# Adding the experts' weighted rows in DRAM by accumulating scatters, in a fused two-layer kernel

## What is computed

```python
logits = flat @ router_w.T                       # 1024 tokens, 32 experts
scores = jnp.sqrt(jax.nn.softplus(logits))
_, idx = jax.lax.top_k(scores + expert_bias, 4)  # four experts per token
topv = jnp.take_along_axis(scores, idx, axis=1)
topv = topv / (topv.sum(axis=-1, keepdims=True) + 1e-20)
...
out = sum over experts e of p[:, e, None] * _clamped_swiglu(flat, gate_w[e], up_w[e], down_w[e])
out = out + _clamped_swiglu(flat, shared_gate_w, shared_up_w, shared_down_w)
```

## Time and profile before

| | before |
|---|---|
| median of 3 runs | 845.72 us (844.31 to 847.45) |
| the profiled execution | 846.73 us |
| its span (first to last instruction) | 844.9 us |
| PE, DVE, ACT, POOL busy | 787.4, 605.4, 465.3, 429.8 us |
| mean granted TensorE clock | 0.993 of full speed |
| read from and written to DRAM | 41.11 MB, 21.86 MB |

### The profile page before, as it was taken

One profiled execution on the slowest core, in us unless ns is written; L12 is line 12 of the kernel. 1 busy time (PEld: TensorE's weight loads), 2 busy tenths in 40 slices (PEclk: granted clock), 3 DMA queues, 4 the chain that ended last, 5 costly groups with the idle time before them and its releaser, 6 DMA issues.

```text
span 844.9 us, 14053 instructions
## 1 busy us (share of the span) xinstructions
PE 787.4 (93%) x4927; PEld 642.0 (76%) x4927; DVE 605.4 (72%) x1069; ACT 465.3 (55%) x822; POOL 429.8 (51%) x487
## 2 busy tenths in 40 slices
PE   7999999998888988899899999999999999999993
PEld 6776776774333376798798899889989999888881
DVE  8588868658999787789788688986777544445544
ACT  4433342379888643786665566556656725555421
POOL 1767837423555455455245435757565415555423
PEclk9999999999999999999999999999999999999997
DMA  5211195000000040000000000101011887543134
GB/s 184 76 38 38 38 288 145 1 1 1 1 1 2 16 132 13 20 11 22 7 19 7 26 7 20 51 25 58 18 46 33 240 303 268 165 133 101 27 101 149
DMA packets 50117, 59.82 MB, mean 71 GB/s; under 512 B 13560, under 2 KB 41085, under 8 KB 50049
## 3 DMA queue, kind: packets, MB, share of 16 engines
q1 hardware_dynamic: 45488, 50.49, 19.4%
q0 software_dynamic: 4560, 8.44, 2.8%
HBM read 41.11 MB, written 21.86 MB: 75 GB/s over the span
## 4 chain that ended last, share of the span: by engine, by line
PE 55%; DVE 9%; ACT 7%; POOL 7%; issue 5%; DMA 1%; SPq 0%; POOLq 0%; ACTq 0%; DVEq 0%
PE ps L801 12%; PE ps L516 8%; PE ps L518 8%; PE ps L517 8%; PE ps L894 4%; PE ps L891 3%; PE ps L925 3%; POOL A L1814 2%; DVE cap L1509 2%; PE ps L712 2%; POOL rot L1845 2%; PE ps L873 1%; PE ps L558 1%; ACT A L1108 1%; DVE swap L1499 1%
## 5 line engine op out<-in xcount | busy, mean ns | idle before, releaser
L801 PE MATMUL ps<-V,P 128*128 128x129 f32 x1152 | 150.7, 276 | 0.0
L1160 ACT ACTIVATE cap<-cap 128x1024 f32<-128x1024 f32 (+7 forms) x128 | 87.1, 681 | 113.7 <-DVE cap L1509 108.1
L801 PEld LDWEIGHTS ps<-V,P 128*128 128x128 f32 x1152 | 143.3, 192 | 2.7
L1509 DVE SCALAR_TENSOR_TENSOR cap<-dist,ps 128x1024 f32<-128x1024 f32 (+7 forms) x128 | 95.4, 750 | 27.9 <-PE ps L518 20.4
L1738 POOL TENSOR_SCALAR_AFFINE_SELECT P<-P 128x128 f32<-128x128 f32 x128 | 39.0, 305 | 144.4 <-ACT P L1165 143.8
L1870 POOL DMA_INDIRECT y_scratch<-y_sb,aux_s x63 | 62.2, 987 | 63.9 <-ACT y_sb L1205 33.7
L1165 ACT ACTIVATE P<-cap 128x1024 f32<-128x1024 f32 (+7 forms) x128 | 87.7, 685 | 4.1
L516 PE MATMUL ps<-q_hi,k_hi 128*128 128x512 f32 x192 | 71.9, 374 | 7.4 <-DVE cap L1509 5.9
L518 PE MATMUL ps<-q_lo,k_hi 128*128 128x512 f32 x192 | 66.9, 348 | 0.0
L517 PE MATMUL ps<-q_hi,k_lo 128*128 128x512 f32 x192 | 66.5, 346 | 0.0
L516 PE MATMUL ps<-xT_hi,w_hi 128*128 128x512 f32 x128 | 56.4, 441 | 2.9 <-POOL w_lo L1758 1.9
(11 more groups left out here) (293 smaller groups left out, 2097.4 us busy)
## 6 DMA issues: line engine op xcount, KB each, us to landing
xg_scratch<-blank SPq DMA_DIRECT2D x1, 8127.0 KB, 31.3
xa<-xg_scratch SPq DMA_DIRECT2D x63, 128.0 KB
ew<-in_experts SPq DMA_DIRECT2D x3, 1920.0 KB, 10.0
y<-y_scratch SPq DMA_DIRECT2D x8, 512.0 KB
pk<-in_packed SPq DMA_DIRECT2D x8, 384.0 KB, 3.1
pks<-in_scales SPq DMA_DIRECT2D x8, 384.0 KB, 4.2
ew<-in_experts SPq DMA_DIRECT2D x1, 3072.0 KB
wqk<-in_wqk SPq DMA_DIRECT2D x20, 128.0 KB
```

The lines of the kernel that those rows point to most:

```text
L801: last = pe.matmul(ps[:, 4 + r % 2, o:o + D1 + 1], P1[:, h % 2, a:a + P], V1[:, j, h // REP, :], start=(j == 0), stop=(j == t))
L1160: act.activation(cap[:, n % 2, 0:w], cap[:, n % 2, 0:w], ACT.Tanh, scale=1.0 / (CAP * float(D1) ** 0.5))\
L1509: dve.scalar_tensor_tensor(out=cap[:, n % 2, 0:w], in0=dist[:, 0:w], scalar=slope, in1=psf[:, 1024 * (n % 2):1024 * (n % 2) + w], op0=ALU. ...
```

## The change

Both arrays are filled with zeros ahead, on SP's queue behind the fill of `xg_scratch`, and POOL's first send waits for all three fills. The index in a row is the token's number. At the end SP loads two rows per token as two DMAs of 128 KB per tile, PE adds both to the shared expert's sum straight from the loaded tile (the pair additions on DVE are gone, and with them the tile `yp`), and the last addition to `x_tok` is on DVE, right behind the product.

```diff
-    y_dram = nc.dram_tensor("y_scratch", (TOPK * TOK, D), F32, kind="Internal").ap()
+    y_dram = [nc.dram_tensor(f"y_scratch{i}", (TOK, D), F32, kind="Internal").ap() for i in range(2)]
...
-        y4 = alloc(l1w)("y4", [P, NT, TOPK, D])
+        y2 = alloc(l1w)("y2", [P, NT, 2, D])
...
+            for i in range(2):
+                sp.dma_start(y_dram[i].rearrange("(b p) d -> p b d", p=P),
+                             blank[:, 0:D].rearrange("p (a d) -> p a d", a=1).to_broadcast((P, NT, D))).then_inc(blank_sent, 16)
...
             for t in range(NT):
-                sp.dma_start(y4[:, t], y_dram.rearrange("(k t p) d -> t p k d", k=TOPK, p=P)[t]).then_inc(in_xg[t], 16)
+                for i in range(2):
+                    sp.dma_start(y2[:, t, i, :], y_dram[i][t * P:(t + 1) * P, :]).then_inc(in_xg[t], 16)
...
             def sum_rows(t):
-                pe.wait_ge(pair_ready, t + 1)
+                pe.wait_ge(in_xg[t], 16 * (len(range(t, NBLK, NT)) + 2))
                 for i in range(2):
-                    last = pe.matmul(sum_at(t), ident[:], pairs_of(t)[:, i, :], start=False, stop=(i == 1))
+                    last = pe.matmul(sum_at(t), ident[:], y2[:, t, i, :], start=False, stop=(i == 1))
...
-                    link(dve.tensor_scalar(xa[:, :, D].bitcast(U32), iota[:, k * NT:(k + 1) * NT], float(P), dist[:, 0:1],
+                    link(dve.tensor_scalar(xa[:, :, D].bitcast(U32), iota[:, 0:NT], float(P), dist[:, 0:1],
...
-            def add_pairs(t):
-                dve.wait_ge(in_xg[t], 16 * (len(range(t, NBLK, NT)) + 1))
-                if t >= 4:
-                    dve.wait_ge(fin_ps, t - 3)
-                dve.tensor_tensor(pairs_of(t), y4[:, t, 0:2], y4[:, t, 2:4], ALU.add).then_inc(pair_ready, 1)
...
+            for t in range(NT):
+                dve.wait_ge(fth_ready, t + 1)
+                dve.tensor_tensor(mix1_b[:, t % 2, :], mix1_a[:, t % 2, :], s_tok[:, t, :], ALU.mult).then_inc(mixed, 1)
+                dve.wait_ge(mixed, NT + t + 1)
+                dve.tensor_tensor(x_tok[:, t, :], x_tok[:, t, :], mix1_b[:, t % 2, :], ALU.add).then_inc(x_ready, 1)
...
-                    pool.wait_ge(blank_sent, 16)
+                    pool.wait_ge(blank_sent, 48)
...
+                if b >= 2:
+                    pool.wait_ge(y_sent[(b - 2) % YRING], 16 * ((b - 2) // YRING + 1))
+                pool.indirect_dma_start(out=y_dram[b % 2], out_offset=bass.IndirectOffsetOnAxis(ap=aux_s[:, b, 0:1].bitcast(U32), axis=0),
+                                        in_=y_sb[:, b % YRING, :], in_offset=None, bounds_check=TOK - 1,
+                                        oob_is_err=False, compute_op=ALU.add).then_inc(y_sent[b % YRING], 16)
...
-            for t in range(NT):
-                pool.wait_ge(mixed, NT + t + 1)
-                pool.tensor_tensor(x_tok[:, t, :], x_tok[:, t, :], mix1_b[:, t % 2, :], ALU.add).then_inc(x_ready, 1)
```

More of the change, by code:

```diff
@@ L280, in build_program @@
         y_sb = sb("y_sb", [P, YRING, D])
-        def pairs_of(t):
-            return yp[:, t % 2] if t % 4 < 2 else gu[:, t % 2].rearrange("p k m n -> p (k m n)").rearrange("p (i d) -> p i d", i=2)
-        yp = sb("yp", [P, 2, 2, D])
         mix1_a = sb("mix1_a", [P, 2, D])
@@ L376, in build_program @@
         y_copied, ws_hi_ready, ws_ready = sem("y_copied"), sem("ws_hi_ready"), sem("ws_ready")
-        pair_ready, fin_ps = sem("pair_ready"), sem("fin_ps")
+        fin_ps = sem("fin_ps")
         vec = sem("vec")
@@ L1869, in send_y @@
                     pool.wait_ge(in_aux, 16)
-                pool.indirect_dma_start(out=y_dram, out_offset=bass.IndirectOffsetOnAxis(ap=aux_s[:, b, 0:1].bitcast(U32), axis=0),
-                                        in_=y_sb[:, b % YRING, :], in_offset=None, bounds_check=TOPK * TOK - 1,
-                                        oob_is_err=False).then_inc(y_sent[b % YRING], 16)
+                if b >= 2:
[3 more added lines that the diff above has]
+                                        oob_is_err=False, compute_op=ALU.add).then_inc(y_sent[b % YRING], 16)
             for step in POOL_STEPS1:
```

## The result

| | before | after |
|---|---|---|
| median of the runs, us | 845.01 (844.3 to 847.45, 4 runs) | 868.55 (866.68 to 871.5, 4 runs) |
| profiled execution, its span, us | 846.73, 844.9 | 866.68, 864.9 |

The ratio is 1.0275, 95% interval 1.0253 to 1.0296: slower by 23 us, where the forecast was faster by 5 (841.0). The upper end of the range, 870, holds it.

What follows compares the result with a forecast made beforehand. TensorE (PE) was taken to bound the experts' phase, and loading, ACT, DVE and POOL the end. -6.2 us at the end and +1.5 for the wait gave -4.7, so 841.0 us against the 845.7 median; range 838.5 to 870.

Steps and rivals of the forecast that it cites:

- the new wait: POOL's scatters, each waiting for the landing of the one two back: 1.5 us of stall in all.
- The zero for the blanking: Two more 1 MB zero fills on SP's queue, about 8 us of idle DMA time: no cost.
- e: Extra time from issue to landing of a scatter because it adds: taken as 0.6 us, counted twice while weights stream.
- The bound from above, 3.6: Most the addition could put on a scatter's landing: a whole load in front of the write, 3.6 us.
- my own bill: Experts' stall by the addition's extra landing time: 3 us at 1, 6 at 1.2 (break-even), 13 at 1.5, 23 at 2.
- The crowded stretch: Scatters while expert weights stream in, from 705.3 us: landing 6.2 us, one scatter per 3.1 us, 1 us of stall.
- The last scatter is as early as before: In 790:815 empty scatters could go one per 1.1 us, so POOL is caught up by the last one.
- The end: After the last scatter: smaller loads, PE sums without DVE pair additions, last addition on DVE; gains 6.2 us.
- The closing stays as it is: Stores and closing of the program, from 836.80 to 844.9 us: unchanged.
- The likeliest case by itself: Whole kernel, with the addition adding up to about 0.9 us to a landing: 839 to 842.5 us, chance 0.46.
- slower by a second trip: Rival: the addition puts a second round trip in each scatter; 852 us, or 862 with more delay; chance 0.27.
- much slower: Rival: each DMA engine's 8 rows of a scatter go one after another, landing 10 us or more; beyond +130 us; chance 0.09.

Runs made afterwards that it cites:

- end_only: Kernel before with only the new end; plain scatters, no wait, only two of each token's four expert rows loaded and summed: 836.05 us, ratio 0.9859.
- after_plain: Kernel after with scatters that do not add, so the sum over a token's experts is left out; all else stays: 841.27 us, ratio 0.994.
- after_one_array: Kernel after with one array instead of two, so every scatter waits for the one before it: 992.54 us (one run).
- after_pool_last: Kernel after with the last addition moved back to POOL (GpSimd): 873.51 us, ratio 1.0334.

## Why the prediction was wrong

**The form was right.** The prediction priced the new wait as a pace of POOL against 1.74 us per block, hidden by four buffers. It named as the sign of failure ACT's copies waiting for scatters and issues over 1.9 us apart; they show 44.2 us and 2.35. The zero for the blanking stands: two more fills cost nothing that shows (start +0.6). So does PE's pace of 0.90 us a tile for the sums (7.07 us for eight in `end_only`).

**The step that failed is the size of e, what the addition adds to the landing L, and the constant beside it.** I wrote (L + 0.1)/2 with L = 2.5 + 0.6, 1.6 us a scatter. Measured: L = 3.9, and 0.8 instead of 0.1, 2.35 us a scatter.
- e is 1.4, not 0.6 (1.2 if set against the 2.7 of `after_plain`). Of it 0.58 is POOL's own writing, 1.56 us instead of 0.98. I had that as a remark under a rival and put nothing of it into e. An empty scatter pays only this: the shortest landings are 2.7 us with the addition (`after_one_array`) and 2.1 without (`after_plain`). The rest, 0.6 to 0.8, comes with the data: 1.1 us of engine time per scatter instead of 0.37, where I had doubled the 0.37. The bound from above, 3.6, held it; what misled me was taking a value from the row of a plain scatter's data, when the addition changes both the descriptors and the size of the packets.
- The 0.8 us from a landing to POOL's next start could be read before: the copy that starts at 700.29 and takes 0.46 is followed by its scatter at 701.53, 0.78 later. I took the 0.1 that an instruction of SP takes.
- In my own bill e = 1.4 stands between 6 and 13 us of stall. With the 0.7 of wake-up, a pace of 2.35, it is e = 2.1 there, some 25 us; the marks show 28. (The bill's own 6 us at e = 1.2 comes to 7.5 when worked again, so the break-even was nearer 1.15; nothing else hangs on it.)

**The crowded stretch was too cheap.** I had L = 6.2 and "1 us of stall". The chain has a landing of 8.26 us for the third scatter and 6.14 for the fifth. In after the 7th scatter is 12.3 us late (723.16 for 710.85), the 44th 33.2 (808.90 for 775.66) and the last 33.3: a good third of the delay is there before the steady pace begins. In `after_plain`, without adding, the 7th is still 10 us late. That is the 5.8 to 9.1 us that the wait costs alone, as much as the predicted gain of the end, at any e.

**"The last scatter is as early as before" was wrong.** I let POOL catch up on empty scatters at 1.1 us each. An adding scatter costs POOL 1.56 + 0.30 = 1.86 us whether or not it moves data; the last one trails its copy by 6.3 us instead of 1.7.

**The end was right on the path.** The predicted -6.2 us are -6.6 in `after_plain` and -6.6 in `end_only` (17.8 against 24.3 in the table). In after only 2.6 are left, since the late scatter and loads that issue in 0.47 us each (7.45/16), not 0.37, put the loads behind PE: its sums wait for them 2.14 us and more.

**"The closing stays as it is" was wrong, in the change's favour.** It lost 6 us, by the move of the last addition off GpSimd, which I had costed only by the two durations. Put back on GpSimd, it makes after 873.51 (`after_pool_last`), though only 2.4 us of the closing return there.

The sum by its terms, as they measured: +28.0 experts (predicted +1.5), -2.6 end (-6.2), -6.0 closing (0), +0.6 start. The likeliest case by itself fell; the case that came is the rival "slower by a second trip", by other means: a slower writing, a dearer transfer and a late wake-up, each under 1 us, in a loop that only two scatters share. That 868.55 still lies under the upper end of the range is in part luck: the 6 us of the closing, which the sum had at zero, brought it there.

The rule of the Trainium skill on packets of one row ("DMA: Bandwidth & Descriptors", section on two DMAs through the same engine) was used only against "much slower", and that did not come: an adding scatter's 8 rows per engine land within 3.9 us, not 10. How the packets follow each other on an engine no run shows.

## What to carry to other kernels

Before making anything wait for a DMA's landing, work out (issue to landing + landing to the next issue)/(transfers in flight), and take the second term from a row of the engine that waits (0.8 us on GpSimd here); if the pace is not clearly below what the stage needs, no buffer will save it, while one more transfer in flight may. An option on a DMA is a new instruction: measure its descriptor writing, its packets and its landing before building on it. When several parts of a change cancel or multiply, run each alone: here everything but the addition was together a small gain, made up of a wait that cost 6 to 9 us and an end and a closing that gave 12, and the largest single gain, one addition moved from GpSimd to VectorE at the end, works on the kernel before as it is (0.990).

## What the runs showed of the hardware

- An indirect scatter of 128 rows of 1 KB that adds: 1.56 us on GpSimd instead of 0.98, median landing 3.8 to 4.3 us (720:775, one to four arrays) instead of 2.7 (`after_plain`), three times the packets (1513 against 500 for 1.10 MB) and three times the DMA time. Scatters whose rows are all out of bounds pay the 1.56 us too.
- From a landing to the start of GpSimd's next scatter: 0.8 us; back to back without a wait: 0.30.
- The closing of the program is 6.0 us shorter (kernel before) or 2.4 us (kernel after, scatters that add) when GpSimd doesn't compute in the last microseconds.
